# Self-attention on one core: GpSimd normalises the first quad of heads before it copies the values and computes the inverse deviation

## The chip, the cores and the metric

The program runs on one core of a Trainium2 chip, as one launch. The time is device microseconds of that core; before the change the median of 3 runs is 837.16 us (836.74 to 841.43). The engines are PE (TensorE, matrix products and transposes), DVE (VectorE), ACT (ScalarE), POOL (GpSimd) and SP (its queue issues most of the DMAs). Each engine works through its own instructions in the order in which they are written, and waits on semaphores for the others.

## The reference, cut to what matters

The reference is one decoder layer on x of shape (2, 1024, 256): windowed self-attention, cross-attention on 77 context rows, and a feed-forward layer with 8 routed experts. The change is in the first part alone:

```
x = x + attn(layernorm(x))
q, k, v = x @ Wq.T, x @ Wk.T, x @ Wv.T          # 16 heads of 16 values
k_pad, v_pad = concat(last_k, k), concat(last_v, v)   # 63 rows ahead of each batch
idx = arange(l)[:, None] + arange(64)[None, :]  # every row sees itself and 63 rows before it
scores = einsum('blhd,blwhd->blwh', q, k_pad[:, idx]) * 16 ** -0.5
attn = softmax(scores, axis=2)
out = einsum('blwh,blwhd->blhd', attn, v_pad[:, idx]) @ Wo.T
```

## The kernel before, in words

x is cut into 16 tiles of 128 rows, 8 for each batch. The self-attention of a tile is spread over three passes of one loop body, `self_attention(i, par, on)`, which every engine has in a version of its own. Body i projects tile i to queries, keys and values, does the scores, exponentials and most of the output of tile i-1, and finishes tile i-2. `sweep_self_attention` (L411 to L427) runs it for i = 0 to 17: bodies 0, 1, 8, 9 and 14 to 17 are written out, and the others are the two halves of hardware loops. `on` says which parts a body has: `on[4]`, the layer-norm statistics of tile i+2, is off from body 14 on, and `on[0]`, everything on a new tile, is off in bodies 16 and 17.

A tile has 16 heads, in four quads of four, numbered 0 to 3. For each quad:

- PE: the scores (L799 the mask, L803 the products) into one half of a PSUM tile.
- DVE `peaks` (L1461): the negated maximum per head, `negm`.
- ACT `exponentials` (L1175): four exponentials with their sums `den`.
- DVE `inverse_sums` (L1470): `rden` = 1 / `den`.
- POOL: the probabilities `prob` times `rden`, in place (L507 for quads 0, 1 and 2 by `normalize(s)`; L513 for quad 3, which comes one body later).
- PE `transposed` (L818): four transposes of `prob`, which wait for that product.
- DVE (quads 0 and 2, L1479) or ACT (quads 1 and 3): the copy `pt` from PSUM to SBUF.
- PE `output` (L837): `pt` times the values.

Within a body, PE's order is: transposes of quad 2 of the tile before, scores 0, the transposes of the next tile's input and the query product, output 2, key product, transposes of quad 3, scores 1, output 3, **transposes of quad 0**, scores 2, value product, transposes of the queries (L775), the product with Wo of the tile before (`oth`, `otl`; L265 to L267), output 0, transposes of quad 1, scores 3, transposes of the keys (L775), output 1. The product with Wo waits for `ol` (POOL's L537) and for `v` (DVE's L1512, the copy of this tile's values out of PSUM).

ACT's order around it is: exponentials 0, the query and key roundings `qs` and `ks` with the copy `pt` of quad 3 between them, `of` (L1203, half of the output of the tile before), `xth`, exponentials 1, exponentials 2. DVE's is: `rden` 0, `qs` (L1492), maximum 1, `ks` (L1351), `whole` (L1501, the other half of the output), `xtl` (L1351), maximum 2, `rden` 1, the values (L1512), `pt` of quad 0, the queries `Q` (L1516), `rden` 2, `xn` (L1424), maximum 3.

POOL's body, which the change reorders, is: product of quad 3 (L513); the copy of 64 rows of the values, from the tile before into `V0` (L523), after which it waits for that copy to end; the inverse deviation of tile i+2 (L489, the power -0.5 of one number per row); product of quad 0 (L507); `oth` and `otl`, the two parts of the output of the tile before (L534, L537); product of quad 1; the copy of the other 64 rows (L547); product of quad 2. The value copy is read by PE's output 0 of the same body, and the inverse deviation by DVE's `xn` in the second half of the body.

SP clears a part of the DRAM buffer `slots` once per tile, when scores 3 of a tile are done. All stages behind the self-attention start when its last tile is added to x (`x1`).

Of the kernel before, what the change touches and what calls it, by code (L numbers as in the profile page):

```python
# [64 lines left out]
def decoder_layer(nc, x, ctx, wq, wk, wv, wo, last_k, last_v, xq, xk, xv, xo, xb,  # L65
# [192 lines left out]
    def sem(name):  # L258
        sems[name] = nc.alloc_semaphore(name)
        return sems[name]  # L260
# [10 lines left out]
    def pass_waits(eng):  # L271

        eng.sem_inc(passed, 1)
# [15 lines left out]
    a = {n: sem("a_" + n) for n in a_names}  # L289
# [23 lines left out]
    C = CREDIT  # L313
# [113 lines left out]
    def quad(i, par, on, s):  # L427


        return C + (i - 1) * 4 + s, on[1], 1 - par  # L430

    @block.gpsimd
    def _(pool):
# [52 lines left out]
        def inverse_deviation(st, s, t):  # L486

            pool.wait_ge(s, C + t * 4 + 3)
            pool.tensor_tensor(st[:, 8:9], st[:, 7:8], minus_half[:, :], ALU.pow).then_inc(s, 1)  # L489
# [12 lines left out]
        def self_attention(i, par, on, starts=0):  # L502
            def normalize(s):
                n, is_on, q = quad(i, par, on, s)
                if is_on:
                    pool.wait_ge(a["rq"], n + 1)
                    pool.tensor_tensor(prob[s][:, :, :], prob[s][:, :, :],  # L507
                                       rden[:, q, 4 * s:4 * s + 4].unsqueeze(2).broadcast_to([P, 4, P]), ALU.mult).then_inc(a["nrm"], 1)

            if on[2]:  # L510
                n, q = C + (i - 2) * 4 + 3, par
                pool.wait_ge(a["rq"], n + 1)
                pool.tensor_tensor(prob[3][:, :, :], prob[3][:, :, :],  # L513
                                   rden[:, q, 12:16].unsqueeze(2).broadcast_to([P, 4, P]), ALU.mult).then_inc(a["nrm"], 1)
            if on[0]:
                first = (starts or type(i) is int and i == 0) and not par
                pool.wait_ge(a["v"], C + i)
                pool.wait_ge(a["pv"], C + (i - 1) * 4 - 2)
                pool.wait_ge(a["ln"], C + i * 4 + (8 if on[3] else 4))
                if on[2]:  # L520
                    pool.wait_ge(a["nrm"], C + (i - 1) * 4)
                pass_waits(pool)
                pool.tensor_copy(V0[par][HB:P, :], (vinit if first else V1[1 - par])[HB:P, :]).then_inc(a["vp"], 1)  # L523
                pool.wait_ge(a["vp"], C + i + 1)
                pass_waits(pool)
            if on[4]:
                inverse_deviation(stats, a["ln"], i + 2)
            if on[1]:
                normalize(0)
            if on[2]:  # L530
                pool.wait_ge(a["of"], C + i - 1)
                pool.wait_ge(a["op"], C + i - 2)
                pass_waits(pool)
                pool.tensor_copy(oth[:, :, :, :], whole[:, :, :, :]).then_inc(a["oh"], 1)  # L534
                pool.wait_ge(a["oh"], C + i - 1)
                pass_waits(pool)
                pool.tensor_tensor(otl[:, :, :, :], whole[:, :, :, :], oth[:, :, :, :].bitcast(F32), ALU.subtract).then_inc(a["ol"], 1)  # L537
            if on[1]:
                normalize(1)
            if on[0]:  # L540
                pool.wait_ge(a["v"], C + i + 1)
                if on[1]:
                    pool.wait_ge(a["nrm"], C + (i - 1) * 4 + 2)
                if on[4]:
                    pool.wait_ge(a["ln"], C + i * 4 + 12)
                pass_waits(pool)
                pool.tensor_copy(V0[par][0:HB, :], V1[par][0:HB, :]).then_inc(a["v0"], 1)  # L547
                pool.wait_ge(a["v0"], C + i + 1)
                pass_waits(pool)
            if on[1]:  # L550
                normalize(2)

        sweep_self_attention(pool, self_attention)

        pool.wait_ge(a["x1"], C + NT)
# [1279 lines left out]
```

## Time and profile before

| | |
|---|---|
| median of 3 runs | 837.16 us |
| profiled execution, its own time | 834.44 us |
| its span, first to last instruction | 832.7 us |
| self-attention, within the span | about 36 to 262 us |
| PE busy, share of the span | 737.1 us, 89% |
| POOL busy, share of the span | 388.0 us, 47% |
| granted TensorE clock, mean | 0.961 |

The profile is one execution. In its timeline each row is one instruction, or several alike in a row (x4), with its start in us from the start of the span, its duration, and in brackets the idle time of the engine before it and the instruction that ended the idle time. PE's rows overlap, as matmuls are pipelined: the engine is free for the next group well before the end of the one before.

### The profile page before, as it was taken

To read this page: it belongs to the slowest core of one execution; us is meant where nothing else is said; L and a number is where in the kernel's file an instruction comes from. 1 tells how busy PE (TensorE), PEld (TensorE's weight loads), DVE (VectorE), ACT (ScalarE), POOL (GpSimd) and SP (SyncE) were. 2 spreads that over 40 slices of the span, in tenths; PEclk is the share of its full clock that TensorE was granted. 3 is DMA by queue.
4 is the path that set the end of the run, shared out by engine and by line. 5 is a ranking of instruction groups with operands and counts; after the bars stand their busy time and mean duration, and the time that the engine had idled before them with its cause. 6 is when DMAs were issued, how large, how long until landed. Compare 5 with 4: busy or idle time off the path is not lost.

```text
span 832.7 us, 18311 instructions
## 1 busy us (share of the span) xinstructions
PE 737.1 (89%) x5593; PEld 664.3 (80%) x5593; DVE 511.1 (61%) x1185; ACT 448.8 (54%) x1599; POOL 388.0 (47%) x398
## 2 busy tenths in 40 slices
PE   4998999999984899999988989999999999986188
PEld 4887778778863788888887979989999999986177
DVE  6767778778762578999974355545554454531146
ACT  2548888888872787677753543333443334422052
POOL 4104555554543455777846920798437300007700
PEclk9999999999996999999998999999999999999579
DMA  8415222122130000000313321365515211113411
GB/s 207 140 39 180 88 102 83 69 103 91 61 115 7 1 1 14 26 31 28 125 48 105 133 83 32 126 205 187 171 38 171 75 38 38 39 39 93 116 39 58
DMA packets 47628, 69.65 MB, mean 84 GB/s; under 512 B 4989, under 2 KB 39317, under 8 KB 47573
## 3 DMA queue, kind: packets, MB, share of 16 engines
q1 hardware_dynamic: 37253, 39.58, 14.7%
q0 software_dynamic: 8576, 29.10, 10.4%
q8 instruction: 29, 0.48, 0.2%
q10 hardware_dynamic: 1744, 0.28, 0.2%
q14 instruction: 26, 0.21, 0.1%
HBM read 40.76 MB, written 28.18 MB: 83 GB/s over the span
## 4 chain that ended last, share of the span: by engine, by line
PE 52%; DVE 12%; issue 8%; ACT 8%; POOL 6%; another core or an unknown queue 5%; DMA 1%; POOLq 0%; DVEq 0%; ACTq 0%; SPq 0%
PE PQ L265 12%; PE PQ L267 11%; PE PQ L266 11%; PE PQ L1061 4%; ACT prob L1250 3%; POOL prob L507 3%; PE PQ L818 2%; PE PQ L775 2%; DVE ptl L1351 2%; PE PQ L997 2%; PE PQ L999 2%; PE PQ L998 2%; DVE hot L1623 2%; PE PQ L803 1%
## 5 line engine op out<-in xcount | busy, mean ns | idle before, releaser
L265 PE MATMUL PQ<-wts,hth 128*128 128x256 f32 x424 | 124.4, 293 | 5.1 <-DVE htl L1351 5.0
L267 PE MATMUL PQ<-wts,htl 128*128 128x256 f32 x424 | 119.7, 282 | 0.0
L266 PE MATMUL PQ<-wts,hth 128*128 128x256 f32 x424 | 119.5, 282 | 0.0
L1351 DVE TENSOR_TENSOR htl<-PQ,hth 128x512 fp32r<-128x512 f32 x106 | 68.9, 687 | 69.2 <-ACT hth L1104 68.5
L1175 ACT ACTIVATE prob<-PQ,negm 128x128 f32<-128x128 f32 x256 | 90.4, 370 | 24.3 <-DVE negm L1461 22.6
L1250 ACT ACTIVATE prob<-PQ,negm 128x77 f32<-128x77 f32 x256 | 79.2, 345 | 39.4 <-DVE negm L1589 39.4
L1104 ACT ACTIVATE hth<-PQ 128x512 fp32r<-128x512 f32 x106 | 58.5, 598 | 77.1 <-PE PQ L1061 77.1
L265 PEld LDWEIGHTS PQ<-wts,hth 128*128 128x128 f32 x424 | 80.8, 191 | 7.6 <-issue 3.8
L266 PEld LDWEIGHTS PQ<-wts,hth 128*128 128x128 f32 x424 | 81.3, 192 | 0.0
L1321 ACT ACTIVATE hact<-PQ 128x512 f32<-128x512 f32 x74 | 44.4, 600 | 67.9 <-DVE PQ L1752 63.2
L267 PEld LDWEIGHTS PQ<-wts,htl 128*128 128x128 f32 x424 | 80.9, 191 | 0.0
L568 POOL TENSOR_TENSOR wts<-raw,wts 128x2048 fp32r<-128x2048 f32 x16 | 73.8, 4610 | 1.4
L1286 ACT ACTIVATE PQ<-PQ,shared_b 128x256 f32<-128x256 f32 x64 | 26.0, 445 | 83.5 <-PE PQ L999 42.2
L1752 DVE TENSOR_TENSOR PQ<-PQ,b_all 128x512 f32<-128x512 f32 x74 | 51.4, 696 | 29.4 <-PE PQ L267 26.5
L1747 DVE TENSOR_TENSOR y_sb<-PQ,b_all 128x256 f32<-128x256 f32 x37 | 15.7, 425 | 78.0 <-PE PQ L267 75.7
L648 POOL DMA_INDIRECT ya<-slots,dest x16 | 15.2, 953 | 103.4 <-DMA slots<-y_sb 98.8
L265 PE MATMUL PQ<-wts,fxh 128*128 128x512 f32 x148 | 62.2, 420 | 1.1 <-DVE fxl L1351 1.1
L507 POOL TENSOR_TENSOR prob<-prob,rden 128x512 f32<-128x512 f32 x48 | 50.9, 1061 | 17.2 <-DVE rden L1470 16.2
L267 PE MATMUL PQ<-wts,fxl 128*128 128x512 f32 x148 | 58.7, 397 | 0.0
L566 POOL CAST wts<-raw 128x2048 fp32r<-128x2048 f32 x16 | 30.5, 1905 | 60.6 <-PE PQ L267 60.5
L266 PE MATMUL PQ<-wts,fxh 128*128 128x512 f32 x148 | 58.4, 394 | 0.0
L489 POOL TENSOR_TENSOR stats<-stats,minus_half 128x1 f32<-128x1 f32 x48 | 26.6, 553 | 68.0 <-DVE stats L1419 61.0
(236 smaller groups left out, 2303.5 us busy)
## 6 DMA issues: line engine op xcount, KB each, us to landing
slots<-zeros SPq DMA_DIRECT2D x16, 1024.0 KB, 4.3
raw<-in_L_ffn_exp_w_dram POOLq DMA_DIRECT2D x16, 1024.0 KB, 5.9
xf_sb<-slots SPq DMA_DIRECT2D x39, 128.0 KB, 2.1
slots<-y_sb SPq DMA_DIRECT2D x37, 128.0 KB, 1.7
b_all<-in_L_ffn_exp_b_dram POOLq DMA_DIRECT2D x6, 512.0 KB, 4.4
raw<-in_L_ffn_shared_w_dram SPq DMA_DIRECT2D x2, 1024.0 KB, 6.8
out_dram<-X SPq DMA_DIRECT2D x16, 128.0 KB
X<-in_x_dram SPq DMA_DIRECT2D x1, 1792.0 KB, 23.4
```

The lines of the kernel that those rows point to most:

```text
L265: pe.matmul(o, lh, rh, start=start, stop=False)
L266: pe.matmul(o, lh, rl, start=False, stop=False)
L267: return pe.matmul(o, ll, rh, start=False, stop=stop)
L507: pool.tensor_tensor(prob[s][:, :, :], prob[s][:, :, :], rden[:, q, 4 * s:4 * s + 4].unsqueeze(2).broadcast_to([P, 4, P]), ALU.mult).then_ ...
L568: pool.tensor_tensor(low, raw[:, cols], high.bitcast(F32), ALU.subtract).then_inc(done, 1)
L1061: last = pe.transpose(down_t[:, n, k * P:(k + 1) * P], hact[:, (4 * n + k) * P:(4 * n + k + 1) * P], ident[:, :])
L1104: return nc.scalar.activation(o, i, ACT.Copy, scale=scale)
L1175: last = nc.scalar.activation(prob[s][:, j, :], self_s[:, s % 2, j * P:(j + 1) * P], ACT.Exp, bias=negm[:, q, u:u + 1], accum_out=den[:, q ...
L1250: last = nc.scalar.activation(prob2[par][:, h, :], ps[:, (h - h0) * CK:(h - h0 + 1) * CK], ACT.Exp, bias=negm2[:, h:h + 1], accum_out=den2 ...
L1321: nc.scalar.activation(hact[:, n * 512:(n + 1) * 512], up[:, n, :], ACT.Gelu).then_inc(f["act"], 1)
L1351: return dve.tensor_tensor(o, whole, high.bitcast(F32), ALU.subtract)
L1752: dve.tensor_tensor(up[:, n, :], up[:, n, :], b1_all[:, e % 2, n * 512:(n + 1) * 512], ALU.add).then_inc(f["add"], 1)
```

## The change

On POOL, the product of quad 0 (`normalize(0)`) moves ahead of the value copy and the inverse deviation. The value copy had a wait for the product of quad 3 (`nrm`, in bodies with `on[2]`); it now waits for the product of quad 0, which is one count further (in bodies with `on[1]`, so in body 1 too). No instruction of work is added or removed, and the other engines' instructions are the same.

```
-                if on[2]:
-                    pool.wait_ge(a["nrm"], C + (i - 1) * 4)
+                if on[1]:
+                    pool.wait_ge(a["nrm"], C + (i - 1) * 4 + 1)
...
             if on[4]:
                 inverse_deviation(stats, a["ln"], i + 2)
-            if on[1]:
-                normalize(0)
```

and ahead of `if on[0]:`, the block of the value copy:

```
+            if on[1]:
+                normalize(0)
             if on[0]:
```

POOL's rows in the second half of the loop's body, before. `prob_98` is quad 3, `prob_95` quad 0; the brackets hold the semaphores for which an instruction waits.

```order
L513 TENSOR_TENSOR prob_98<-prob_98,rden 128x512 [waits a_rq]
L518 REGISTER_ALU [waits a_v]
L519 ISA [waits a_pv]
L521 REGISTER_ALU [waits a_ln]
L523 COPY V_1_88<-V_0_89 64x256 [waits a_nrm]
L524 REGISTER_ALU
L488 ISA [waits a_vp]
L489 TENSOR_TENSOR stats<-stats,minus_half 128x1 [waits a_ln]
L506 REGISTER_ALU
L507 TENSOR_TENSOR prob_95<-prob_95,rden 128x512 [waits a_rq]
L534 CAST oth<-whole 128x256 [waits a_of,a_op]
```

The same place now:

```order
L513 TENSOR_TENSOR prob_98<-prob_98,rden 128x512 [waits a_rq]
L506 REGISTER_ALU
L507 TENSOR_TENSOR prob_95<-prob_95,rden 128x512 [waits a_rq]
L520 REGISTER_ALU [waits a_v]
L521 ISA [waits a_pv]
L525 COPY V_1_88<-V_0_89 64x256 [waits a_ln,a_nrm]
L526 REGISTER_ALU
L488 ISA [waits a_vp]
L489 TENSOR_TENSOR stats<-stats,minus_half 128x1 [waits a_ln]
L534 CAST oth<-whole 128x256 [waits a_of,a_op]
```

The product of quad 0 now stands right behind that of quad 3, and the copy and the power stand between it and `oth`.

In body 14, which has no inverse deviation, POOL's rows before are:

```order
L513 TENSOR_TENSOR prob_98<-prob_98,rden 128x512 [waits a_rq]
L523 COPY V_0_87<-V_1_90 64x256 [waits a_nrm,a_ln,a_v,a_pv]
L507 TENSOR_TENSOR prob_95<-prob_95,rden 128x512 [waits a_vp,a_rq]
L534 CAST oth<-whole 128x256 [waits a_of,a_op]
L537 TENSOR_TENSOR otl<-whole,oth 128x256 [waits a_oh]
```

and now:

```order
L513 TENSOR_TENSOR prob_98<-prob_98,rden 128x512 [waits a_rq]
L507 TENSOR_TENSOR prob_95<-prob_95,rden 128x512 [waits a_rq]
L525 COPY V_0_87<-V_1_90 64x256 [waits a_nrm,a_ln,a_v,a_pv]
L534 CAST oth<-whole 128x256 [waits a_vp,a_of,a_op]
L537 TENSOR_TENSOR otl<-whole,oth 128x256 [waits a_oh]
```

Only the copy changes places with the product there, and the wait for the copy's end is now `oth`'s.

## Rows read from the trace of the kernel before

**Rows 1.** Waits in 70:220 us, who waited for whom: total, times, longest
```profile
PE PQ L818 <- POOL prob L507: 7.4, 12, 0.6
```

**Rows 2.** Chain that ended last, body 11: start, us, what
```profile
183.80 1.05 POOL prob L513
...
185.03 0.38 POOL V L523
...
185.66 0.54 POOL stats L489
186.21 1.02 POOL prob L507
...
187.34 0.65 PE PQ L818 x4
```

**Rows 3.** Timeline of PE, bodies 11 and 12
```profile
182.12 0.39 PE L799 MATMUL PQ<-window,identb 128*128 128x512 bf16 x1
...
186.28 0.42 PE L837 MATMUL PQ<-pt,V 128*32 128x128 f32 x8
...
190.03 0.36 PE L265 MATMUL PQ<-WTh,oth 128*128 128x256 f32 x1
...
194.44 0.39 PE L799 MATMUL PQ<-window,identb 128*128 128x512 bf16 x1
...
202.35 0.35 PE L265 MATMUL PQ<-WTh,oth 128*128 128x256 f32 x1
...
206.74 0.39 PE L799 MATMUL PQ<-window,identb 128*128 128x512 bf16 x1
```

**Rows 4.** Timeline of DVE, body 11
```profile
185.28 0.18 DVE L1470 RECIPROCAL rden<-den 128x4 f32<-128x4 f32 x1 [0.73 <-ACT prob L1175]
185.77 0.42 DVE L1492 SCALAR_TENSOR_TENSOR qs<-PQ,qs 128x256 f32<-128x256 f32 x1 [0.31 <-ACT qs L1104]
...
186.82 0.41 DVE L1351 TENSOR_TENSOR ks<-PQ,ks 128x256 f32<-128x256 f32 x1
187.36 0.48 DVE L1501 SCALAR_TENSOR_TENSOR whole<-PQ,owner,of 128x256 f32<-128x256 f32 x1
187.76 0.41 DVE L1351 TENSOR_TENSOR xtl<-PQ,xth 128x256 fp32r<-128x256 f32 x1
188.64 0.69 DVE L1461 TENSOR_REDUCE negm<-PQ 128x4 f32<-128x512 f32 x1 [0.47 <-PE PQ L803]
189.25 0.17 DVE L1470 RECIPROCAL rden<-den 128x4 f32<-128x4 f32 x1
189.50 0.43 DVE L1512 COPY V<-PQ 128x256 f32<-128x256 f32 x1
...
191.91 0.39 DVE L1424 TENSOR_SCALAR xn<-X,stats 128x256 f32 x1
```

**Rows 5.** Timeline of POOL, body 11
```profile
188.04 0.40 POOL L534 CAST oth<-whole 128x256 fp32r<-128x256 f32 x1 [0.82 <-DVE whole L1501]
188.61 0.73 POOL L537 TENSOR_TENSOR otl<-whole,oth 128x256 fp32r<-128x256 f32 x1 [0.18 <-POOL oth L534]
...
192.07 1.12 POOL L507 TENSOR_TENSOR prob<-prob,rden 128x512 f32<-128x512 f32 x1 [0.84 <-DVE rden L1470]
```

**Rows 6.** Timeline of ACT, bodies 11 and 12, the last sums of exponentials 1
```profile
188.76 0.23 ACT L1175 ACTIVATION_READ_ACCUMULATOR prob<-PQ,negm 128x1 f32 x1
...
201.12 0.23 ACT L1175 ACTIVATION_READ_ACCUMULATOR prob<-PQ,negm 128x1 f32 x1
```

**Rows 7.** Timeline of DVE, body 14
```profile
225.84 0.18 DVE L1470 RECIPROCAL rden<-den 128x4 f32<-128x4 f32 x1
225.93 0.41 DVE L1512 COPY V<-PQ 128x256 f32<-128x256 f32 x1
```

**Rows 8.** Timeline of PE, body 14
```profile
226.44 0.35 PE L265 MATMUL PQ<-WTh,oth 128*128 128x256 f32 x1
```

**Rows 9.** Timeline of POOL, body 1
```profile
63.00 1.04 POOL L507 TENSOR_TENSOR prob<-prob,rden 128x512 f32<-128x512 f32 x1 [0.45 <-DVE rden L1470]
```

## The prediction

> **What bounds the kernel now.** I read the waits of the self-attention first. PE, the busiest engine, has one wait that comes back in every body: its transposes of quad 0 wait for POOL's product of quad 0, 7.4 us in 12 bodies (2 to 13), 0.6 us each [rows 1]. The chain of waits then shows what stood ahead of that product on POOL: the product of quad 3, the value copy, the inverse deviation, and only then the product, after which PE starts [rows 2]. The question is when the product's own input was there. DVE's `rden` 0 ends at 185.28 + 0.18 = 185.46, while the product starts at 186.21 [rows 4, 2]. So it is late by its queue alone.
>
> The body has a fixed length: from scores 0 to the next scores 0 it is 194.44 - 182.12 = 12.32 us and 206.74 - 194.44 = 12.30 us [rows 3].
>
> **The change, step by step,** in body 11; the others are alike.
>
> The product of quad 0 now follows quad 3's, which ends at 184.85 [rows 2], and waits for `rden` 0 until 185.46. DVE's `rden` 1 is followed by its reader on its own engine after 0.08 us (189.42 to 189.50), and I take 0.1 us here: start 185.56, end at 1.02 us more, 186.58. PE followed the product after 187.34 - 187.23 = 0.11 us, so its transposes start at 186.69 if PE is free. Output 3 ahead of them ends at 186.28 + 0.42 = 186.70 [rows 3], so PE is free just then. The step is worth 187.34 - 186.70 = **0.64 us**, practically the whole wait of 0.6 us.
>
> The value copy and the inverse deviation come behind it. The copy starts 0.18 us after the product (as after quad 3's), takes 0.38, the power follows 0.25 us later and takes 0.54 [rows 2]: 186.58 + 1.35 = 187.93. Next in POOL's queue is `oth`, which started at 188.04, 0.20 us after `whole` ended at 187.84 [rows 4, 5]. I put it at 188.04 to 188.1: the 0.82 us in which POOL sat idle, with the time won ahead, takes them. Their readers are far away: the inverse deviation's is `xn` at 191.91, 4 us later; the copy's is output 0, behind the product with Wo at 190.03. Both cost nothing; the cover is this idle time, and without it each 0.1 us would reach `oth`, `otl` and the product with Wo.
>
> Now what is late next. With PE 0.64 us earlier, the product with Wo could start at 190.03 - 0.64 = 189.39. It waits for two things.
> - `otl`: ends at 188.61 + 0.73 = 189.34, or 189.4 with `oth` at 188.1, and PE follows 0.1 us later: 189.5.
> - The values' copy on DVE. It stands behind `rden` 1, which needs the last sum of exponentials 1, and these stand in an ACT queue that scores 0 and output 3 set, not quad 0. That sum ends at 188.99 [rows 6]. Body 14, where no inverse deviation stood ahead of the product, shows the distances when this is tight: `rden` to values 0.09 us, values 0.41, values to PE 226.44 - 226.34 = 0.10 [rows 7, 8]. With 0.05 from the sum to `rden`, my guess at a hop that is no longer than the other two, 188.99 + 0.05 + 0.09 + 0.43 + 0.10 = 189.66. DVE's maximum 2, ahead of `rden` 1, doesn't hold it: it waited 0.47 us for PE's scores and may start when `xtl` ends at 188.17, which puts `rden` 1 at 188.8.
>
> So the product with Wo starts at 189.66 instead of 190.03: 0.37 us. In body 12 the last sum ends at 201.35, the same sum gives 202.02 against 202.35 [rows 3, 6]: 0.33 us. From there to the next scores 0 there were 4.41 and 4.39 us of PE's work, and everything on DVE and ACT in that stretch follows PE's scores, so that it moves along. **0.35 us a body in 12 bodies is 4.2 us.**
>
> The bodies at the ends. In body 1 the product waited for `rden` itself [rows 9]: nothing. In bodies 14 and 15 only the copy stood ahead, and the values' copy already sets the start of the product with Wo, to 0.10 us [rows 7, 8]: 0 to 0.1 us together. Bodies 16 and 17 have nothing moved.
>
> Everything behind the self-attention starts with the last tile's sum and is tied to it by semaphores, SP's clearing of `slots` too. I carry the 4.2 us through unchanged. The profiled execution, 834.44 us with a span of 832.7, becomes 830.2. It lies 2.7 us below the median of the runs, 837.16, and from this I take off the same: **833.0 us**, 0.5% faster.
>
> **Rivals.**
>
> *Nothing is late next: the whole wait goes.* 12 x 0.62 = 7.4 us, 829.8 us. For it: the waits view shows no other wait of PE that large [rows 1]. Against it: the sum of exponentials 1 at 188.99, which nothing in the change moves. It would need the queries' and values' path on ACT and DVE to shorten as well. 12%.
>
> *The time is given back.* The value-copy wait, or `oth` behind the inverse deviation, comes 0.2 to 0.4 us later than I have it. The distances between POOL's instructions, 0.18 and 0.25 us, are waits for its own results, and the body now has them between the product of quad 0 and `oth`. If `oth` starts at 188.3, `otl` ends at 189.6, and PE gains 0.3; at 188.5 it gains 0.1 or nothing. Gain 0 to 3 us, 834.2 to 837.2. 22%.
>
> *Slower: the product meets DVE's work.* It used to run beside DVE's maximum 1 and `ks`; it now runs from 185.56 to 186.58, over `qs` at 185.77. If the two cannot read at once and DVE waits until POOL is done, `qs` starts at 186.6 instead of 185.77, and maximum 1, `ks` and `whole` come 0.8 us later; `whole` then ends at about 188.6, `oth` starts at 188.8, `otl` ends at 190.1 and the product with Wo starts at 190.2 instead of 190.03, 0.2 us later than before. That is 12 x 0.2 = 2.4 us slower, 839.6 us. It decides from about 0.6 us of delay on DVE, with less it only eats the gain. Against it: before, the product (186.21 to 187.23) ran beside `ks` at 186.82, which like `qs` reads PSUM and SBUF, and `ks` took its 0.41 us [rows 4]. For it: there is one pair that does disturb each other. POOL's product of quad 2 at 192.07 overlaps `xn` (191.91 to 192.30), SBUF to SBUF, and takes 1.12 us instead of 1.04 [rows 4, 5]; 0.08 us, not 0.6. 7%.
>
> The Trainium skill, page "SBUF — State Buffer", section "SBUF: two separate sides", says that GpSimd and a DVE instruction with two SBUF inputs, or in a two-port mode, lock each other out for the whole instruction. By that rule `xn`, if it runs in such a mode, would have held the product back until 192.30, by 0.23 us; the trace shows 0.08. The rule does not cover `qs`, with one SBUF input, and by it this rival would be worth nothing.
>
> *The change does not do what it says.* The product comes earlier, but PE's transposes are held by output 3, which waits for ACT's `pt`. Then the gain of the first step is smaller. Output 3 ends at 186.70 and the product, with its hop, would be ready at 186.69, so the two meet already. Even if output 3 held PE for 0.3 us more, PE would still be at Wo by 189.69, when the values are ready: it costs nothing up to there, and lies inside my own case.
>
> **How the numbers follow.** My forecast 56%, the whole wait 12%, given back 22%, slower 7%, and 3% for something behind the self-attention, such as another course of the granted clock. My own case goes from 0.25 to 0.45 us a body, 3.0 to 5.4 us: 831.8 to 834.2. Faster than 829.2 I leave out: it is the whole wait and half a microsecond. At the top the range goes to no change at all, 837.2, and leaves out the slower case. A measurement of this kernel can't tell less than about 1%, 8.4 us, from no change. No case reaches that: the largest gain is 7.4 and the loss 2.4. So within 1% has 93%; faster by more than that, below 828.8, has 5%, as it lies next to the whole wait; slower has 2%.
>
> **What the profile of the changed kernel would show.** The product of quad 0 starts 0.1 us after `rden` 0, 3.4 us after scores 0 instead of 4.1. PE's wait for it shrinks from 0.6 us to below 0.1. The product with Wo gets a wait of 0.2 to 0.3 us, ended by DVE's values or POOL's `otl`, and PE's maskings L799 come every 11.95 us instead of 12.31. `oth` starts within 0.1 us of its former place, 5.92 us after scores 0. I am wrong if that product has no wait (then the gain is larger), if `oth` starts later than 6.2 us after scores 0 (then smaller), or if `qs` on DVE starts later than 3.8 us after scores 0.

## The result and the profile after

The changed kernel takes 834.22 us (median of 20 runs) against 837.32 us for the kernel before (20 runs), a ratio of 0.9952 with a 95% interval of 0.9934 to 0.9969: 3.1 us faster by the medians, 4.0 us by the ratio, 2.6 to 5.5 us by its interval. The forecast was 833.0 us, 4.2 us faster.

The profiled execution of the changed kernel does not show this at first sight. Its span is 834.6 us, longer than the 832.7 us of the execution before. Whoever compares the two spans gets the wrong sign, so I cut both at the scores 0 of each body (first score product of PE, L803) and took the length of each stretch:

| stretch, us | before | after | difference |
|---|---|---|---|
| start of the span to scores 0 of body 1 | 58.66 | 63.61 | +4.95 |
| body 1 | 12.29 | 13.90 | +1.61 |
| **bodies 2 to 13** | **148.13** | **143.62** | **-4.51** |
| body 14 to scores 3 of body 16 | 32.41 | 32.29 | -0.12 |
| from there to the end | 581.21 | 581.18 | -0.03 |

The change moves instructions in bodies 1 to 15. The first row, the loading of the inputs and weights, lies outside it. The last row says that in this pair what the self-attention won was handed on to the end. How close it comes is chance: over three profiles of each kernel that stretch took 578.7 to 581.2 us before and 578.5 to 581.2 us after the change, with means of 579.6 and 579.8 us. So it neither adds nor takes more than the 2 to 3 us by which it varies by itself.

The waits of the changed kernel in 70:220 us, who waited for whom (total, times, longest); only those of PE's transposes and of its product with Wo:

```profile
PEld PQ L265 <- POOL otl L537: 3.2, 12, 0.3
...
PEld PQ L818 <- POOL prob L507: 0.4, 2, 0.2
```

(PEld is PE's loading of weights.) The 7.4 us of [rows 1] are gone, and a wait that wasn't there stands in front of the product with Wo, in all 12 bodies. Body 11 in the timeline, PE:

```profile
185.27 0.39 PE L799 MATMUL PQ<-window,identb 128*128 128x512 bf16 x1
...
189.43 0.43 PE L837 MATMUL PQ<-pt,V 128*32 128x128 f32 x8
189.86 0.65 PE L818 MATMUL PQ<-ident,prob 128*128 128x128 f32 x4
...
192.80 0.36 PE L265 MATMUL PQ<-WTh,oth 128*128 128x256 f32 x1
...
197.22 0.39 PE L799 MATMUL PQ<-window,identb 128*128 128x512 bf16 x1
```

DVE:

```profile
188.43 0.18 DVE L1470 RECIPROCAL rden<-den 128x4 f32<-128x4 f32 x1 [0.73 <-ACT prob L1175]
188.92 0.42 DVE L1492 SCALAR_TENSOR_TENSOR qs<-PQ,qs 128x256 f32<-128x256 f32 x1 [0.31 <-ACT qs L1104]
...
190.51 0.48 DVE L1501 SCALAR_TENSOR_TENSOR whole<-PQ,owner,of 128x256 f32<-128x256 f32 x1
...
192.18 0.18 DVE L1470 RECIPROCAL rden<-den 128x4 f32<-128x4 f32 x1 [0.26 <-ACT prob L1175]
192.28 0.42 DVE L1512 COPY V<-PQ 128x256 f32<-128x256 f32 x1
```

ACT, the last sum of exponentials 1:

```profile
191.92 0.23 ACT L1175 ACTIVATION_READ_ACCUMULATOR prob<-PQ,negm 128x1 f32 x1
```

POOL:

```profile
188.69 1.04 POOL L507 TENSOR_TENSOR prob<-prob,rden 128x512 f32<-128x512 f32 x1 [0.70 <-DVE rden L1470]
189.89 0.40 POOL L525 COPY V<-V 64x256 f32<-64x256 f32 x1 [0.16 <-PE PQ L837]
190.54 0.55 POOL L489 TENSOR_TENSOR stats<-stats,minus_half 128x1 f32<-128x1 f32 x1 [0.26 <-POOL V L525]
191.19 0.40 POOL L534 CAST oth<-whole 128x256 fp32r<-128x256 f32 x1
191.77 0.73 POOL L537 TENSOR_TENSOR otl<-whole,oth 128x256 fp32r<-128x256 f32 x1 [0.18 <-POOL oth L534]
```

Against [rows 2 to 5]: the product of quad 0 starts 0.08 us after `rden` 0 and 3.42 us after scores 0; PE's transposes start the moment output 3 ends (189.86). The values' copy ends at 192.70, and the product with Wo starts at 192.80, 7.53 us after scores 0; it was 190.03 - 182.12 = 7.91. `otl` ends at 192.50. The waits view names `otl`, but what came last by these rows is the values' copy, 0.10 us ahead of PE. The body takes 197.22 - 185.27 = 11.95 us.

The other half of the loop differs in one point that body 11 doesn't show. In the even bodies `whole` starts 5.37 us after scores 0 instead of 5.23, in both kernels, and `oth` and `otl` come 0.2 us later with it (`oth` at 6.10 instead of 5.91). Body 12 of the changed kernel, whose scores 0 are at 197.22:

```profile
203.91 0.73 POOL L537 TENSOR_TENSOR otl<-whole,oth 128x256 fp32r<-128x256 f32 x1 [0.18 <-POOL oth L534]
```

```profile
204.26 0.42 DVE L1512 COPY V<-PQ 128x256 f32<-128x256 f32 x1
```

```profile
204.79 0.36 PE L265 MATMUL PQ<-WTh,oth 128*128 128x256 f32 x1
```

There `otl` ends at 204.64 and the values at 204.68, only 0.04 us apart.

In the chain of waits of the whole program, POOL's share went from 6% to 1%, before and after:

```profile
PE 52%; DVE 12%; issue 8%; ACT 8%; POOL 6%; another core or an unknown queue 5%; DMA 1%; POOLq 0%; DVEq 0%; ACTq 0%; SPq 0%
```

```profile
PE 55%; DVE 14%; ACT 10%; issue 6%; another core or an unknown queue 5%; DMA 1%; POOL 1%; SPq 0%; DVEq 0%; ACTq 0%; POOLq 0%
```

### The profile page after: what moved, and what is told of

Its sections match the earlier page's. It is cut to its first block, busy times and chain, and to the rows that moved or that the text cites. A ratio compares the mean times of both kernels' runs of the same rounds, so it can differ in the third digit from the quotient of the medians.

```text
span 834.6 us, 18301 instructions
## 1 busy us (share of the span) xinstructions
PE 745.8 (89%) x5593; PEld 669.3 (80%) x5593; DVE 510.8 (61%) x1185; ACT 448.2 (54%) x1599; POOL 388.8 (47%) x398
## 4 chain that ended last, share of the span: by engine, by line
PE 55%; DVE 14%; ACT 10%; issue 6%; another core or an unknown queue 5%; DMA 1%; POOL 1%; SPq 0%; DVEq 0%; ACTq 0%; POOLq 0%
PE PQ L265 12%; PE PQ L267 11%; PE PQ L266 11%; ACT prob L1250 4%; PE PQ L1061 4%; PE PQ L818 3%; PE PQ L775 3%; ACT prob L1175 3%; PE PQ L803 2%; PE PQ L837 2%; DVE ptl L1351 2%; PE PQ L799 2%; DMA xf_sb<-slots 1%; DVE negm L1589 1%
## 5 line engine op out<-in xcount | busy, mean ns | idle before, releaser
L1250 ACT ACTIVATION_READ_ACCUMULATOR prob<-PQ,negm 128x1 f32 x256 | 58.6, 229 | 0.0
```

Of the source, the lines that this page charges most:

```text
L1250: last = nc.scalar.activation(prob2[par][:, h, :], ps[:, (h - h0) * CK:(h - h0 + 1) * CK], ACT.Exp, bias=negm2[:, h:h + 1], accum_out=den2 ...
```

## The experiments

My theory: (a) the product of quad 0 was late by POOL's queue alone; (b) what limits the gain is the values' copy on DVE, behind the sums of exponentials 1; (c) what the 12 bodies win is the whole difference. The rivals: every operation ahead of the product costs its own time; `otl` is the new limit, as the waits view says; or the time is given back further on.

As runs of one kernel spread over 7 to 13 us, the sum of the bodies 2 to 13 in the profile is the finer measure. Over six profiles of the two kernels it repeated to 0.2 us. Each experiment is read by both. Where the text turns a ratio into us, it is the ratio times the kernel before; the difference of the medians is said beside it where it is another.

| kernel | bodies 2 to 13, us | ratio to before, 95% interval |
|---|---|---|
| before, again | 147.94 | 1.0013 (0.9991 to 1.0035) |
| before, third time | 148.03 | 0.9978 (0.9956 to 0.9999) |
| changed, again | 143.51 | 0.9948 (0.9919 to 0.9976) |
| changed, third time | 143.60 | 0.9925 (0.9888 to 0.9962) |
| power alone behind the product | 143.76 | 0.9954 (0.9924 to 0.9984) |
| copy alone behind the product | 143.66 | 0.9963 (0.9940 to 0.9985) |
| changed, values ahead of `rden` 1 | 142.07 | 0.9935 (0.9907 to 0.9963) |
| before, values ahead of `rden` 1 | 148.02 | 0.9982 (0.9957 to 1.0007) |
| changed, load ahead of the product | 143.52 | 0.9973 (0.9944 to 1.0003) |
| changed, load behind it | 145.75 | 0.9972 (0.9946 to 0.9998) |
| changed, two loads behind it | 152.38 | 1.0125 (1.0074 to 1.0176) |
| the same, again | 152.38 | 1.0055 (1.0028 to 1.0081) |

### Both kernels again

No edit. Expected of the kernel before:

> The kernel before, once more, as the measure of what differs with no change at all. Both theories: ratio to the kernel before 1.000 within its interval. In the profile the bodies 2 to 13 take 12.31 us each (148.1 us from scores 0 of body 2 to scores 0 of body 14), and the rest of the span may differ by some microseconds in the loading of the inputs and in body 1, where PE waits 2.6 us and the granted clock may fall or not.

and of the changed one:

> The changed kernel once more, beside the kernel before on the same chip. Theory (0.37 us won in each of 12 bodies, passed on unchanged): 4.4 us faster, ratio 0.995, bodies 2 to 13 take 143.6 us together. Rival (the wait is given back and the measured difference is chance): ratio 1.000, and the 12 bodies take 148 us.

Measured: 147.94 us and 143.51 us for the 12 bodies, ratios 1.0013 and 0.9948. The theory holds, and the difference is no chance.

### Half of the change: only the inverse deviation goes behind

```
-            if on[4]:
-                inverse_deviation(stats, a["ln"], i + 2)
             if on[1]:
                 normalize(0)
+            if on[4]:
+                inverse_deviation(stats, a["ln"], i + 2)
```

> Of the change only one half: the inverse deviation goes behind the product of quad 0, the value copy stays ahead of it. Theory: what counts is when POOL is free against when rden 0 is there. Quad 3's product ends 0.6 us before rden 0 does, the copy takes 0.56 us with its gap, so it fits into the wait; the product starts at most 0.1 us later than in the changed kernel, and the product with Wo is set by DVE's values anyway. Bodies of 11.95 us, 4.4 us faster than before, the same as the changed kernel. Rival (each thing that stands ahead costs its own time): the copy costs its 0.6 us, only half of the gain is left, bodies of 12.1 us, 2 us faster.

Measured: 143.76 us, ratio 0.9954. POOL and DVE's `rden` 0 in body 11, whose scores 0 are at 182.49:

```profile
184.16 1.04 POOL L513 TENSOR_TENSOR prob<-prob,rden 128x512 f32<-128x512 f32 x1 [2.90 <-DVE rden L1470]
185.37 0.40 POOL L523 COPY V<-V 64x256 f32<-64x256 f32 x1 [0.17 <-POOL prob L513]
186.00 1.04 POOL L507 TENSOR_TENSOR prob<-prob,rden 128x512 f32<-128x512 f32 x1 [0.24 <-DVE rden L1470]
```

```profile
185.65 0.18 DVE L1470 RECIPROCAL rden<-den 128x4 f32<-128x4 f32 x1 [0.73 <-ACT prob L1175]
```

The copy stands ahead of the product, and the bodies are as short as with both moved. But it isn't quite `rden` 0 that the product waits for, as the bracket has it. `rden` 0 ends at 185.83 and the product starts 0.17 us behind it, where the changed kernel has 0.08; it starts 0.23 us behind the end of the copy, and POOL waits for that end before it goes on (0.25 us from copy to power in the changed kernel). So, as expected, the copy still holds the product by 0.1 us, and the transposes stand 187.18 - 182.49 = 4.69 us after scores 0 instead of 4.59. That 0.1 us is taken by PE's wait in front of the product with Wo, which starts at 7.54 us, as in the changed kernel.

### The other half: only the value copy goes behind

Against the changed kernel, cut to what moves (`nrm` is waited for as in the changed kernel):

```
+            if on[4]:
+                inverse_deviation(stats, a["ln"], i + 2)
             if on[1]:
                 normalize(0)
             if on[0]:
                 ...
-            if on[4]:
-                inverse_deviation(stats, a["ln"], i + 2)
```

The value copy then also waits for the inverse deviation (`ln`, four counts further).

> The other half: the value copy goes behind the product of quad 0, the inverse deviation stays ahead of it. Theory: the power needs 0.55 us and fits between quad 3's product and rden 0 as well, if its input is there; DVE's statistics end 0.3 us before quad 3's product does. It starts 0.1 us after quad 3's product and ends about when rden 0 does: bodies of 11.95 to 12.0 us, 4 to 4.4 us faster than before. Rival (each costs its own time): 0.8 us ahead of the product, bodies of 12.1 to 12.2 us, 1.5 to 2 us faster.

Measured: 143.66 us, ratio 0.9963.

```profile
185.03 1.04 POOL L513 TENSOR_TENSOR prob<-prob,rden 128x512 f32<-128x512 f32 x1 [2.94 <-DVE rden L1470]
186.03 0.55 POOL L489 TENSOR_TENSOR stats<-stats,minus_half 128x1 f32<-128x1 f32 x1
186.78 1.04 POOL L507 TENSOR_TENSOR prob<-prob,rden 128x512 f32<-128x512 f32 x1 [0.20 <-DVE rden L1470]
```

The power fits into the wait, with 0.20 us to spare: `rden` 0 ended at 186.70, and the product follows it after 0.08 us, as in the changed kernel. Against 148.03 us, the mean of the three profiles of the kernel before, each half alone brings 4.3 to 4.4 us, and both together 4.5. Two operations of 0.6 us each stood in a wait of 0.7 us; one of them was free, or all but free, whichever it was. The rival that each costs its own time falls.

### The values ahead of `rden` 1, on the changed kernel

On DVE:

```
+            if on[0]:
+                ... dve.tensor_copy(V1[par][:, :], self_v) ...
             inverse_sums(1)
-            if on[0]:
-                ... dve.tensor_copy(V1[par][:, :], self_v) ...
```

> The changed kernel, and on DVE the copy of the values out of PSUM stands ahead of rden 1 instead of behind it. Theory (the product with Wo waits for the values, and these for the sums of exponentials 1): the values' copy starts when PE's value product is done, 0.25 to 0.3 us earlier; then POOL's otl is what comes last, 0.15 to 0.2 us before today's start. Bodies of 11.8 us instead of 11.97, 2 us faster than the changed kernel, ratio to before 0.993. rden 1 comes 0.2 us later, and with it the product of quad 1, which has that room. Rival (otl is what comes last, as the waits view of the changed kernel says, or rden 1 being later is paid at the transposes of quad 1): bodies of 11.95 us or longer, no gain or a loss.

Measured: 142.07 us, 1.5 us less than the changed kernel where I had expected 2, ratio to before 0.9935. Most bodies alternate, 11.71 us in the odd and 11.91 us in the even ones. One of the longer ones, body 12, POOL and then PE:

```profile
198.30 0.40 POOL L534 CAST oth<-whole 128x256 fp32r<-128x256 f32 x1 [0.29 <-DVE whole L1501]
198.88 0.73 POOL L537 TENSOR_TENSOR otl<-whole,oth 128x256 fp32r<-128x256 f32 x1 [0.18 <-POOL oth L534]
```

```profile
199.66 0.39 PE L265 MATMUL PQ<-WTh,oth 128*128 128x256 f32 x1
```

Here `otl` ends at 199.61 and PE follows 0.05 us later: now it is `otl`. In the changed kernel it was the values, since moving them alone shortened the bodies. The odd ones, but for body 7 (0.07 us), got 0.20 to 0.24 us shorter: there `otl` had been ready 0.20 us before the values, and the waits view had named the wrong one of the two. The even ones got only 0.04 to 0.09 us shorter, because `otl` stands right behind the values there. So the values set the gain of the change, but in every second body `otl` is a second limit at nearly the same place. This version is the shortest in its bodies of all that ran, by 6.0 us against before. Against the changed kernel the runs, whose intervals overlap, can't tell it apart.

### The same edit on the kernel before

> The kernel before, with POOL's old order, and on DVE the copy of the values ahead of rden 1. Theory (before the change the bodies are set by the product of quad 0, and DVE's values follow PE's value product by 0.1 us already): no difference from before, bodies of 12.31 us, perhaps some hundredths longer as rden 1 is later. Rival (the values' place on DVE is worth something by itself): bodies shorter by 0.1 us or more, over 1 us faster than before.

Measured: 148.02 us, ratio 0.9982. Nothing, as the theory has it: while POOL's product holds the transposes of quad 0, PE reaches the product with Wo no sooner than the values are there. The same edit is worth 1.5 us behind the change and nothing ahead of it.

### A load on POOL, behind and ahead of the product

A copy of 128x512 numbers that nobody reads, in bodies 2 to 13:

```
+            if on[2] and on[4]:
+                pool.tensor_copy(idle_out[:, :, :], zeros[:, :].unsqueeze(1).broadcast_to([P, 2, D]))
```

Ahead of `oth`:

> The changed kernel with a copy of 128x512 numbers that nobody reads, some 0.8 us on POOL, between the inverse deviation and oth, in bodies 2 to 13. Theory (behind the product of quad 0 POOL has no room left, since oth starts as soon as both the power and whole are there): oth, otl and the product with Wo come about 0.8 us later, less the 0.2 us for which otl had been there before the values: 0.6 us a body, 7.5 us slower than the changed kernel and 3 us slower than before. Rival (POOL has room there, it is busy half of the time): no difference from the changed kernel.

Measured: 145.75 us, 2.1 us more than the changed kernel, where I had expected 7.5; ratio 0.9972, still faster than before. POOL, DVE and PE in one body that began at 182.5:

```profile
187.79 0.55 POOL L490 TENSOR_TENSOR stats<-stats,minus_half 128x1 f32<-128x1 f32 x1 [0.26 <-POOL V L526]
188.29 0.62 POOL L532 COPY idle_out<-zeros 128x512 f32<-128x512 f32 x1
188.85 0.40 POOL L537 CAST oth<-whole 128x256 fp32r<-128x256 f32 x1
189.43 0.73 POOL L540 TENSOR_TENSOR otl<-whole,oth 128x256 fp32r<-128x256 f32 x1 [0.18 <-POOL oth L537]
```

```profile
189.53 0.42 DVE L1515 COPY V<-PQ 128x256 f32<-128x256 f32 x1
```

```profile
190.21 0.39 PE L266 MATMUL PQ<-WTh,oth 128*128 128x256 f32 x1 [0.19 <-POOL otl L540]
```

Two sizes in my expectation were off. The copy occupies POOL for 188.85 - 188.29 = 0.56 us, not 0.8, and `oth` was 0.4 us later in the odd bodies, since it had not started before 5.92 us anyway, and 0.2 us in the even ones, where it had not before 6.10. `otl` ends at 190.16 behind the values at 189.95, and PE follows it by 0.05 us. So in this odd body about 0.25 us of the 0.4 were free; in the even ones it was 0.1 of 0.2. The ordinary bodies paid about 0.15 us each, 8 and 9 nearly 0.3. What I had left out is the room ahead of `oth`, so that the theory's "no room left" was not quite so; the direction was right, the size less than a third.

Ahead of the product of quad 0:

> The same copy that nobody reads, but between quad 3's product and the product of quad 0. Theory (there POOL waits 0.7 us for rden 0 in each body): the product of quad 0 starts 0.1 to 0.3 us later, and the product with Wo, set by the values, has 0.25 us of room for that: 0 to 0.1 us a body, 0 to 1.2 us slower than the changed kernel. Rival (POOL's load costs the same wherever it stands): 0.6 us a body, as with the copy behind it.

Measured: 143.52 us, no difference from the changed kernel. Its ratio, 0.9973 (0.9944 to 1.0003), lies above that of the changed kernel, and the bodies don't explain it; the intervals overlap, and in its profile the stretch behind the self-attention was the longest of all, 582.7 us.

```profile
186.81 1.04 POOL L514 TENSOR_TENSOR prob<-prob,rden 128x512 f32<-128x512 f32 x1 [2.91 <-DVE rden L1473]
187.79 0.61 POOL L517 COPY idle_out<-zeros 128x512 f32<-128x512 f32 x1
188.55 1.04 POOL L508 TENSOR_TENSOR prob<-prob,rden 128x512 f32<-128x512 f32 x1
```

The product still starts 0.08 us behind the end of `rden` 0 (188.47), not 0.1 to 0.3 us later as expected. The same 0.6 us of POOL cost nothing in one place and 2.1 us in the other.

Two loads ahead of `oth`:

> The changed kernel with two copies that nobody reads between the inverse deviation and oth, where one made the 12 bodies 2.1 us longer together. One such copy occupied POOL for 0.56 us and put oth 0.4 us later. Theory (the product with Wo may see otl 0.2 to 0.25 us later before it costs, and from there on each 0.1 us on POOL costs 0.1 us): the second copy puts oth 0.56 us later still, all of it on the path: 12 bodies of 12.65 us, 152.4 us instead of 145.7 and 143.6, and 3 to 4 us slower than before the change. Rival (the first copy cost something else, such as a port of the memory): the second costs as much as the first, 0.15 us a body, 147.8 us.

Measured: 152.38 us, and 12.66 us in an ordinary body, as the theory said. Past the point where `otl` decides, each 0.1 us on POOL costs 0.1 us. The ratio was 1.0125 though, 10 us, where the bodies give 4.3. This ran on another chip, on which both kernels are 34 to 38 us shorter (before: 799.39 us), and only 4 runs stood against 7. The profile puts that difference behind the self-attention: from scores 3 of body 16 to the end it took 544.9 us, and 580.6 us in the later profile of the same kernel. So I ran it once more, beside both kernels.

> The kernel before, beside the changed one and the one with two loads. It tells whether 10 us, which the kernel with two loads was slower than the one before on a chip where both are 36 us shorter, belong to the 12 bodies (4.3 us by their profile) or to the stages behind them. Both theories: ratio 1.000, bodies 2 to 13 148.0 us.

> The changed kernel for the third time. Theory (what the bodies win is the whole difference): 143.6 us for the 12 bodies and 4.5 us less in all, ratio 0.9945. Rival (the stages behind add to it or take from it): the 12 bodies as said, and the total differs from before by less than 2 or more than 7 us.

> The kernel with two loads once more. Theory (the bodies are all of it): 152.4 us for the 12 bodies and 4.4 us slower than before, ratio 1.005. Rival (something behind the self-attention is slower as well, as the 10 us of the run before this one say): ratio 1.01 or more, with the time outside the bodies longer than in the kernel before.

Measured: the kernel with two loads 152.38 us and 1.0055, which is 4.6 us (6.6 by the medians, 2.3 to 6.8 by the interval) for the 4.4 of the bodies; the changed kernel 143.60 us and 0.9925, 6.3 us (4.6 by the medians, 3.2 to 9.4 by the interval) against 4.4; the kernel before 148.03 us and 0.9978. The bodies repeat, and the totals agree with them as far as their intervals of 4 to 6 us can tell. What made the 10 us on the other chip I did not settle; no profile of the kernel before was taken there.

## Why the prediction was right

- *The product of quad 0 was late by its queue alone.* Right. It starts 0.08 us behind `rden` 0, where I had 0.1. The source of that 0.1 was no source: the values' copy, which follows `rden` 1 on DVE, reads PSUM and not `rden`. The figure came right by luck; body 1, where the product waits for `rden` 0 itself, has it, 63.00 - 62.92 = 0.08 us. The two halves sharpen the rest: the product was 0.67 us later than its input allowed; moving the copy takes all of that, moving the power all but 0.1 us, which another wait covers.
- *PE wins 0.64 us there.* Right: the transposes stand 189.86 - 185.27 = 4.59 us after scores 0, and stood 187.34 - 182.12 = 5.22, 0.63 us later.
- *The copy and the power cost nothing.* Right: `oth` stands at 5.92 us after scores 0, as before. The one-load kernel shows the room behind it: in body 11 a delay is paid from 0.25 us on, in the even bodies from 0.1 us. "The others are alike" did not hold there, and in this change it cost nothing, as `oth` did not move in either half.
- *Next comes the values' copy, the product with Wo 0.37 us earlier in body 11 and 0.33 in body 12.* Right: 7.53 us after scores 0, where the forecast has 189.66 - 182.12 = 7.54. In body 12 it was 7.57 against 7.90, the 0.33. The steps are those of the sum: the last sum of exponentials 1 ends 6.88 us after scores 0 (6.87 before), `rden` 1 starts 0.03 us later, where I had guessed 0.05, the copy 0.10 us after that and takes 0.42, and PE follows after 0.10. The values-first kernel shows that it was the copy.
- *0.35 us a body, 4.2 us in all.* The 12 bodies won 4.51 us. The ten ordinary ones went from 12.28 to 12.32 us down to 11.91 to 11.98, 0.35 us each. The other two, bodies 8 and 9 at the seam of the batches, went from 12.70 and 12.42 to 12.25 and 11.82, 0.45 and 0.60; I had taken them to be like the others. That is the 0.3 us missing from the sum. Of the 0.60 some 0.15 us are chance: in the two other profiles of the kernel before, body 9 took 12.25 and 12.28 us. In both bodies the product with Wo came 0.44 us earlier (7.84 to 7.40 us after scores 0), as the transposes of quad 0 came 0.7 us earlier and the values were ready sooner there.
- *Bodies 14 and 15 win 0 to 0.1 us.* Nearly. Body 14, whose rows the forecast is from, won nothing (11.78 and 11.81 us). Body 15 won 0.14 us (11.73 and 11.59), and so it did in the two repeats, by 0.15 us: before the change PE started its product with Wo 0.17 us behind the values there, so that they did not set it.
- *Everything behind is handed on.* Right within what the runs tell, which is 2 to 3 us in one profile. The -0.03 us of the two profiles is luck. The three comparisons of the two kernels by their runs give 4.0, 4.4 and 6.3 us, each with an interval that holds the 4.5 us of the bodies.
- *A measurement can't tell less than about 1%.* Too wide: 20 runs against 20 gave an interval of 0.35%, which leaves 1 out.

Of the rivals, the whole wait going would have needed bodies of 11.7 us; the values-first kernel reaches that in every second one, so the limit that spoke against it was the real one. Given back: `oth` did not come later. Slower by a meeting with `qs` on DVE: `qs` starts 0.49 us after `rden` 0 and takes 0.42 us, in both kernels.

## What to carry to other kernels

An operation that stands in an in-order queue ahead of a critical one costs only what it pushes that one past its own inputs; take the end of the latest input, not the sum of the durations ahead, and test each piece alone before moving all of them. If the engine waits for an operation's own end before it goes on, that wait counts as part of the operation. The gain of a removed wait ends at the next wait, so follow the engine to its next two or three semaphores and write down when each of their producers is done. Where a change of half a percent is wanted from runs that spread by 1.5%, cut the profile at a landmark that recurs and compare the period.

## What the runs showed of the hardware

**The same wait in the same place, with and without a fall of the clock.** In body 1, PE waits 2.60 us for the product [rows 9]. The execution of the kernel before kept full clock through it, the one of the changed kernel did not. The granted clock (third value from the right, after the busy times) in stretches of 4 us, first of the kernel before, then of the changed one:

```profile
64.00:68.00 4.00, 3.46 (x33) 3.02 (x34) 3.32 (x8) 3.33 (x18) 1.46 (x3) 1.00 0.93 275
```

```profile
68.00:72.00 4.00, 2.74 (x12) 2.62 (x13) 2.18 (x5) 2.53 (x11) 1.95 (x3) 0.66 0.92 259
```

and the four transposes behind the wait, in the same order:

```profile
64.30 0.63 PE L818 MATMUL PQ<-ident,prob 128*128 128x128 f32 x4 [2.60 <-POOL prob L507]
```

```profile
69.26 1.04 PE L818 MATMUL PQ<-ident,prob 128*128 128x128 f32 x4 [2.60 <-POOL prob L507]
```

0.66 as a mean lies between 1.2 GHz (0.5) and 2.4 GHz (1.0); in 70:72 us it is 0.50. Body 1 was 1.6 us longer with it. It isn't the change: one of the three profiles of the kernel before has body 1 at 14.74 us, with a granted clock of 0.50 in 66:70 us behind the wait, and two of the three of the changed kernel have it at 12.3, with 1.00 throughout. What decides between the two is open; PE's wait was 2.59 to 2.64 us in all of these.

**Identical kernels do not always compare as equal.** The kernel before against itself gave 1.0013 (0.9991 to 1.0035) and 0.9978 (0.9956 to 0.9999); the second interval ends just short of 1. Verdicts of 0.2% from such intervals are not safe; scores 0 of body 1, ahead of any effect, came between 58.3 and 63.7 us in the profiles of one program and the other.

**POOL and DVE do disturb each other, by part of an instruction.** In the kernel before, `xn` was under way when POOL's product began, and the product took 1.12 us instead of 1.04 [rows 4, 5]. In bodies 14 and 15, which have no `xn`, the same product takes 1.04 us. In the kernel with two loads, POOL's value copy began 0.03 us behind `xn`, and it is `xn` that got longer, 0.57 us instead of 0.39, while the copy kept its 0.39:

```profile
184.76 0.57 DVE L1429 TENSOR_SCALAR xn<-X,stats 128x256 f32 x1
```

```profile
184.79 0.39 POOL L552 COPY V<-V 64x256 f32<-64x256 f32 x1 [0.31 <-POOL prob L509]
```

In the body behind it the two began a little further apart, the copy 0.08 us behind `xn` (197.45 and 197.37), and there it was the copy that took 0.56 us and `xn` kept its 0.39. None of these shows one of the two standing still until the other was done: `xn` would then have taken some 0.8 us, an estimate from 0.39 for each. I did not try this by itself.
